# Moving the skip path of the next slot forward in VectorE's order, to the place behind the second conv tap and scan

## The reference, cut to what matters

```
x = x + 0.5 * ffn(layernorm(x))
x = x + mamba2(layernorm(x))          # 64 heads of 64 channels, state 128
x = x + 0.5 * ffn(layernorm(x))

mamba2:  gate, hbc, dt = split(x @ in_proj_w)
         x, B, C = split(silu(causal_conv4(hbc) + conv_b))
         Y_diag  = within a chunk: (C B^T * decay * dt) @ x
         states  = per chunk:      (decay to its end * dt * B)^T x
         prev    = scan over chunks: new = chunk_decay * prev + states
         Y_off   = C @ prev * exp(cum)
         hidden  = (Y_diag + Y_off + D * x) * silu(gate)      # "+ D * x": the skip path
         out     = rmsnorm(hidden) * norm_w @ out_proj_w
```

## Time and profile before

| what | value |
|---|---|
| median of the runs | 1499.91 us |
| the profiled execution | 1502.24 us |
| its span, first to last instruction | 1500.5 us |
| PE busy | 1385.1 us (92%) |
| DVE busy | 1119.6 us (75%) |
| ACT busy | 1038.7 us (69%) |
| POOL busy | 637.2 us (42%) |

### The profile page before, as it was taken

One profiled execution on the slowest core, in us unless ns is written; L12 is line 12 of the kernel. 1 busy time (PEld: TensorE's weight loads), 2 busy tenths in 40 slices (PEclk: granted clock), 3 DMA queues, 4 the chain that ended last, 5 costly groups with the idle time before them and its releaser, 6 DMA issues. The chain is left out here.

```text
span 1500.5 us, 26270 instructions
## 1 busy us (share of the span) xinstructions
PE 1385.1 (92%) x8704; PEld 1088.5 (73%) x8704; DVE 1119.6 (75%) x2675; ACT 1038.7 (69%) x2133; POOL 637.2 (42%) x639
## 2 busy tenths in 40 slices
PE   4889977768999999999999999999999999987998
PEld 4777766556777777777777777777777777764887
DVE  6853444675888888888888888888888888886433
ACT  1124333576898888889888888988888898871332
POOL 1013211023555565656556555655655565561000
PEclk9999989888999999999999999999999999996999
DMA  5220000224445554344454534555543554334000
GB/s 125 71 88 25 15 15 14 68 45 95 114 96 112 125 106 121 98 107 109 109 128 106 110 100 106 117 110 121 114 104 92 119 121 107 98 86 182 15 14 28
DMA packets 102080, 136.37 MB, mean 91 GB/s; under 512 B 27744, under 2 KB 49856, under 8 KB 101824
## 3 DMA queue, kind: packets, MB, share of 16 engines
q1 hardware_dynamic: 99840, 132.67, 37.0%
q10 hardware_dynamic: 2112, 2.10, 0.4%
HBM read 124.76 MB, written 9.96 MB: 90 GB/s over the span
## 5 line engine op out<-in xcount | busy, mean ns | idle before, releaser
L1008 POOL TENSOR_TENSOR hid<-hid,sg 128x512 f32<-128x512 f32 x128 | 209.1, 1634 | 328.2 <-DVE hid L1277 328.2
L845 ACT ACTIVATE M<-cum_row,cum_table 128x128 f32<-128x128 f32 x1024 | 311.9, 389 | 0.0
L1215 DVE SCALAR_TENSOR_TENSOR xs<-psum,conv_w_sb,xs 128x509 f32<-128x509 f32 (+2 forms) x384 | 285.1, 742 | 0.4
L1611 PE MATMUL psum<-hid,wo 128*128 128x512 f32 x512 | 243.1, 597 | 9.4 <-ACT eT L756 9.2
L989 POOL TENSOR_TENSOR M<-M,CB 128x512 f32<-128x512 f32 x128 | 164.3, 1284 | 115.6 <-ACT M L853 115.6
L1269 DVE TENSOR_TENSOR psum<-psum,e_row 128x512 f32<-128x512 f32 x128 | 89.5, 700 | 145.4 <-PE psum L1584 145.4
L997 POOL TENSOR_TENSOR squares<-squares,sq 128x512 f32<-128x512 f32 x124 | 162.3, 1309 | 2.7 <-ACT sq L822 2.7
L1611 PEld LDWEIGHTS psum<-hid,wo 128*128 128x128 f32 x512 | 96.2, 189 | 84.4 <-issue 72.7
L1596 PE MATMUL psum<-M,xdt 128*64 128x128 f32 x2048 | 140.1, 279 | 0.9 <-DVE psum L1269 0.9
L1570 PE MATMUL psum<-xend,B_tok 128*128 128x128 f32 x1024 | 137.6, 278 | 0.0
L853 ACT ACTIVATE M<-M 128x1024 f32<-128x1024 f32 x128 | 134.5, 1050 | 0.5
(11 more groups left out here) (202 smaller groups left out, 3081.6 us busy)
## 6 DMA issues: line engine op xcount, KB each, us to landing
cum_row<-cum_scratch SPq DMA_DIRECT2D x256, 256.0 KB, 4.5
e_row<-e_scratch SPq DMA_DIRECT2D x256, 128.0 KB, 3.5
xw_raw<-L_attn_in_proj_w_dram SPq DMA_DIRECT2D x32, 128.0 KB, 3.1
wo_raw<-L_attn_out_proj_w_dram SPq DMA_DIRECT2D x32, 128.0 KB, 3.2
gw_raw<-L_attn_in_proj_w_dram SPq DMA_DIRECT2D x16, 256.0 KB, 6.7
x_res<-_attn_hidden_states_dram ACTq DMA_DIRECT2D x4, 512.0 KB, 9.9
x_scratch<-x_res SPq DMA_DIRECT2D x4, 512.0 KB, 2.6
x_res<-x_scratch SPq DMA_DIRECT2D x1, 2048.0 KB, 7.7
```

Of the source, the lines that this page charges most:

```text
L845: last = nc.scalar.activation(M[:, v % 3, h, c * CH:(c + 1) * CH], cum_row[:, v % 2, h, c * CH:(c + 1) * CH], ACT.Relu, bias=scalar_of(CUM ...
L1008: nc.gpsimd.tensor_tensor(hid[:, v % 2, :], hid[:, v % 2, :], sg[:, v % 8, :], ALU.mult).then_inc(hid_done, 1)
L1215: nc.vector.scalar_tensor_tensor(xs[:, v % 8, shift:], psum[:, X_BANK + v % 2, 0:TT - shift], tap_of(v, step), xs[:, v % 8, shift:], ALU.m ...
L1611: last = nc.tensor.matmul(psum[:, OUT_BANK + m, :], wo[:, j, m * P:(m + 1) * P], hid[:, v % 2, :], start=(j == 0), stop=(j == GP - 1))
```

## The change

Three lines of VectorE's order move; nothing else is touched. `skip_path(s + 1)` now stands behind `scan(s+2, 1)` and ahead of `conv_tap(s+7, 2)`. It moves past one conv tap, two scans and the two multiplications with `dt` and with the decay to the chunk's end. `skip_path` issues one instruction and no DMA; its waits and its semaphore are the same.

```
                     conv_tap(s + 7, 1)
                 if alive(s + 2):
                     scan(s + 2, 1)
+                if alive(s + 1):
+                    skip_path(s + 1)
                 if alive(s + 7):
                     conv_tap(s + 7, 2)
                 if alive(s + 2):
                     scan(s + 2, 2)
                 if alive(s + 3):
                     times_dt(s + 3)
                     to_chunk_end(s + 3)
                 if alive(s + 2):
                     scan(s + 2, 3)
-                if alive(s + 1):
-                    skip_path(s + 1)
                 if alive(s + 2):
                     masked(s + 2)
                     scale_off(s + 2)
```

## The result

The changed kernel takes 1478.88 us, median of 4 runs (1475.89 to 1480.79), against 1500.08 us of the kernel before on the same chip (1498.86 to 1502.32): a ratio of 0.9856, 95% interval 0.9845 to 0.9868, or 21.2 us less. 1475.7 was forecast. The profiled execution went from 1502.24 us (span 1500.5) to 1480.27 us (span 1478.6).

What follows compares the result with a forecast made beforehand. PE was taken as the bound, pausing where off waits for the skip path. Gains of 19.3 (steady part), 4.4 (loop's end) and 0.5 (start) sum to 24.2 us: 1499.91 to 1475.7 us, range 1472.5 to 1484.

Steps and rivals of the forecast that it cites:

- Steady part: 117 slots of the loop: off released early enough behind add_out, each slot 7.945 us, gain 19.3 us, between 10 and 19.4.
- Lead 0.31 us: the tightest place: In slots behind add_out, scan 3 would end at 901.06, 0.31 us before states is due at 901.37; no loss taken.
- The 9 us kept for it: Allowance in the range for states coming late in 29 slots, at worst 0.3 us in each.
- rival 1: Behind add_out, states waiting for scan 3 or scale_off held by the port lock costs 9 to 18 us; chance 0.13.
- skip_path waits for diag: At its new place in VectorE's order, skip_path would find diag ended 0.55 us earlier in iterations without add_out.
- Rival 3: Slower: skip blocks VectorE because diag ends later, and each delays the other; decides at 1.6 us; chance 0.03.
- The port pair: VectorE's masked and GpSimd's instructions lock each other out; masked could lose 1.03 us, against 1.05 us spare: no loss.
- Sum 4.4: Gain in us at the loop's ending slots: 1.58 from an earlier off, then 1.4, 0.9 and 0.5.
- Full clock behind the remaining 1.61 us pause: Near the loop's end, PE was taken to keep full clock behind 1.7 us of pause; a fall would cost 1.6 us.
- the slot after the last but one add_out took 6.20 and goes to 5.3: One slot near the loop's end would shorten from 6.20 to 5.3 us, a gain of 0.9 us.
- up to 0.25 us more each: Short slots at the loop's end, no longer ended by the skip, would lose this much further; 0.5 us for three.
- At the start ... 0.5: Second slot's off no longer waits 0.53 us for the skip: gain taken as 0.5 us, between 0 and 0.7.

Runs made afterwards that it cites:

- e1: The change with skip_path at its new place only in iterations following an add_out, old place in the other three of four: 1481.25 us, against 1501.28 before.
- e2: The change with skip_path at its old place behind add_out and at the new place in the other three iterations of four: 1502.08 us, against 1501.28 before.
- e6: The change with skip_path one place later, behind the last tap and scan 2, ahead of times_dt: 1475.65 us, against 1499.93 before.
- e9: The change with skip_path two places later, behind times_dt: 1477.98 us, against 1502.22 before.
- e10: The change with skip_path later still, behind to_chunk_end and ahead of scan 3: 1492.87 us, against 1502.22 before.
- e5: The change with skip_path further up, first in VectorE's iteration, ahead of the first conv tap: 1543.84 us, against 1499.93 before.
- e7: The change up to iteration 120; from 121 VectorE runs scans 0 to 2, skip, masked, times_dt, to_chunk_end, scan 3: 1479.05 us, against 1499.93 before.
- e4: The change with GpSimd's second mask and addition of squares cut to 8 columns from 512 in the last slots: 1475.55 us, against 1501.28 before.
- e8: The changed kernel itself, run again unaltered: 1478.13 us, against 1499.93 before.
- e11: The change with skip_path behind scan 2, the same kernel as e6, with more rounds: 1475.17 us, against 1502.22 before.

## Why the prediction was right, and where it was off

By its own steps, against the profiled executions (21.9 us of span gained, 24.2 forecast). The steady part, four fifths of the sum, was right in cause and size. The total came so near partly by luck, for the loop's end gave 3.3 us less than its term and the start 2.0 us more:

- "Steady part: 117 slots at 7.945, gain 19.3 us": 19.16 us measured. Cause and place as foreseen, shown by e1 and e2, and the size of the release that is needed by e6, e9 and e10. The 0.67 us a slot lump two slots together: before the change 17.1 us were lost in the 29 slots behind an add_out and 2.2 in the slots after them (8.02 us each). The release computed at 899.48 against an off at 900.48 was 887.54 against 888.52.
- "Lead 0.31 us: the tightest place" (scan 3 before states): it cost nothing. 888.64 + 0.47 = 889.11 against 889.42, again 0.31 us; e5 and e7 show that this is what bites next. The 9 us kept for it, and rival 1, did not come.
- "skip_path waits for diag" (0.55 us of lead): no wait in the steady part. Rival 3 named a real circle, but closed it mainly through the wrong wait. I let it decide 1.6 us from the row. By that e5, which brings VectorE to the skip 2.3 us earlier, would cost 0.7 us a slot against the change; it costs 0.46, most of it through scan 3 and states, not through scale_off.
- The port pair: masked met the gate 15 times in the steady part, at 1.70 to 1.73 us and at no cost, 8 times in the slot that was named (the one after the slot behind add_out) and 7 times one slot further on. The failed step is that this was weighed for the steady part only.
- "Sum 4.4" for the loop's end: 37.19 - 36.10 = 1.09 us. The first of its parts held: the off of slot 122 came after 6.93 us instead of 8.61, 1.68 us (1.58 forecast). Full clock behind the remaining 1.61 us pause held too: no window of the end reads below 1.00. The next slot took 6.01 where 5.6 was taken, since states waited 0.51 us for scan 3. But "the slot after the last but one add_out took 6.20 and goes to 5.3" and "up to 0.25 us more each" failed: the last four slots, which would have taken 20.2 us by the sum, took 23.16. e4 gives 2.3 us of it to GpSimd meeting masked, scan 3 ahead of states shows in slot 124 (0.3 us), and the rest is not shown. This is the term that was too large.
- "At the start ... 0.5": this term was too small. The wait of 0.53 us before the off of slot 1 is gone, but from the off of slot 0 to that of slot 4 it is 57.56 us instead of 60.06, 2.50 less; e2 and e8 repeat it, and e1, with the skip at its old place in most of these iterations, has 59.50. Part of it shows as clock: between the offs of slots 2 and 3 the granted clock was 0.98 instead of 0.88, and they lie 8.14 us apart instead of 9.00. How the rest divides is not shown. Slot 0 itself came 1.03 us later, which is scatter. The last stage was 0.2 us shorter.

19.16 + 1.09 + 2.50 - 1.03 + 0.18 = 21.9 us. By the medians 21.2 us were gained of the 24.2.

## What to carry to other kernels

Ask which of the bounding engine's waits ends last and by how much it is late against the undisturbed period; a release that comes 0.4 us early is worth exactly as much as one 1.0 us early, so move the instruction no further than the deadline needs. An instruction that itself waits for the bounding engine closes a circle when it stands too early: put independent work ahead of it, as scan 2 in e6. And do the sums for the first and the last iterations on their own, where the cover of the steady state is missing.

## What the hardware showed beside this

- masked on VectorE and GpSimd's two-input instructions, all of them with their operands in SBUF, exclude each other, and the first to start keeps the other waiting to its end: masked 0.69 us alone, 1.71 when it began 0.12 us behind the gate; the gate 1.27 us alone and 1.65 when masked had begun first (median before, 1.29 after). The Trainium skill, SBUF — State Buffer, "Who interferes with whom", says so, and these numbers agree; it makes the order of two idle-looking engines a cost at 0.1 us of difference.
- The prediction had no row to tell whether the clock falls behind a pause of 1.7 us; the runs have. All of them pause before the off of slot 122, and there the granted clock over the next 4 us was 1.00 behind pauses of 1.61 us (the change), 1.70 (e11) and 1.71 (e6). It was 0.57 behind 2.04 us (e5) and 2.30 (e9), 0.61 behind 2.90 (e10) and 0.57 behind 3.28 (before). So the last six slots of e5, e9 and e10 contain a stretch at 1.2 GHz, and those of the change do not. The windows view of the change, e6 and e5, in the columns of the earlier trace rows:

```profile
1300.74:1304.74 4.00, 3.49 (x36) 3.16 (x36) 3.58 (x10) 3.97 (x11) 0.25 (x1) 1.00 0.05 18
...
1298.58:1302.58 4.00, 3.55 (x36) 3.15 (x36) 3.88 (x12) 3.97 (x9) 1.21 (x1) 1.00 0.16 51
...
1361.25:1365.25 4.00, 4.00 (x20) 3.87 (x20) 2.82 (x6) 3.97 (x11) 0.00 (x0) 0.57 0.06 19
```
